# Decoder block on one core: a bias split on 16 rows, and the rounding of x1 moved from GpSimd to ScalarE

## The reference, cut to what matters

```python
def _L0_xattn_ref(q, k, v):
    ...
    scores = jnp.einsum('bkgsd,bktd->bkgst', qh, kh) / scale
    weights = jax.nn.softmax(scores, axis=-1)
    out = jnp.einsum('bkgst,bktd->bkgsd', weights, vh)
    ...
def _L0_ffn_ref(inputs, ln_w, ln_b, W1, b1, W2, b2):
    ...
    def mx_linear(x, W, b):
        y = jnp.einsum('btk,ok->bto', mx_quant(x), mx_quant(W))
        return bf16_round(y + b)
    ...
    h = mx_layernorm(x, ln_w, ln_b)
    h = mx_linear(h, W1, b1)
    h = mx_gelu(h)
    h = mx_linear(h, W2, b2)
    return bf16_round(residual + h)
x = _layernorm(x + _L0_attn_ref(x, ...), axis=-1)
x = _layernorm(x + _L0_xattn_ref(x, ctx_512, ctx_512), axis=-1)
x = _layernorm(x + _L0_ffn_ref(x, ...), axis=-1)
```

## Time and profile before

| what | value |
|---|---|
| time, median of 3 runs | 302.58 us (300.61 to 304.55) |
| the profiled execution | 303.54 us |
| its span in the trace | 301.7 us |
| busy, PE (TensorE matmuls) | 272.9 us, 90% |
| busy, DVE (VectorE) | 271.9 us, 90% |
| busy, ACT (ScalarE) | 223.0 us, 74% |
| busy, POOL (GpSimd) | 186.3 us, 62% |
| granted clock of TensorE | 1.00 of full speed |

### The profile page before, as it was taken

The page is one execution under the profiler, slowest core; times in us unless marked ns, Lnnn a source line. Parts: engine busy times, 40 slices in busy tenths (PEclk is TensorE's granted clock), DMA queues, the critical chain, the costliest instruction groups (busy, mean ns, idle before and its releaser), DMA issues.

```text
span 301.7 us, 5413 instructions
## 1 busy us (share of the span) xinstructions
PE 272.9 (90%) x1692; PEld 165.8 (55%) x1707; DVE 271.9 (90%) x665; ACT 223.0 (74%) x364; POOL 186.3 (62%) x255
## 2 busy tenths in 40 slices
PE   7898897889798999999999999999788888998887
PEld 2675556547636674667566756674346343534443
DVE  3799999999989989998999899989995999889893
ACT  4130465485898879898999899989988898875551
POOL 2829578478655768786877687767675355522321
PEclk9999999999999999999999999999999999999999
DMA  8940021102003000101210111010000000000101
GB/s 222 381 106 1 0 68 40 35 10 63 1 2 104 0 2 0 36 3 39 69 35 1 46 61 35 3 49 25 9 0 2 35 1 15 22 2 0 37 36 37
DMA packets 10067, 12.30 MB, mean 41 GB/s; under 512 B 2995, under 2 KB 7347, under 8 KB 9782
## 3 DMA queue, kind: packets, MB, share of 16 engines
q1 hardware_dynamic: 9606, 11.16, 11.9%
q10 hardware_dynamic: 432, 0.79, 0.7%
HBM read 9.85 MB, written 2.10 MB: 40 GB/s over the span
## 4 chain that ended last, share of the span: by engine, by line
PE 49%; DVE 27%; ACT 12%; issue 6%; POOL 3%; DMA 1%; DVEq 0%; POOLq 0%; ACTq 0%
PE bank L2041 9%; PE bank L2066 8%; PE bank L2079 7%; DVE am L1351 5%; DVE nm L1265 4%; PE bank L1975 3%; PE bank L2001 3%; PE bank L2145 3%; PE bank L2120 3%; ACT p_sb L848 2%; DVE wam L1351 2%; ACT xT L841 2%; ACT y_sb L862 2%; PE bank L2118 2%; ACT L848 2%
## 5 line engine op out<-in xcount | busy, mean ns | idle before, releaser
L1265 DVE TENSOR_REDUCE nm<-bank 128x4 f32<-128x512 f32 x128 | 84.1, 679 | 6.1 <-PE bank L2041 5.0
L848 ACT ACTIVATE p_sb<-bank 128x512 f32<-128x512 f32 x128 | 71.9, 599 | 13.3 <-PE bank L2066 12.5
L2041 PE MATMUL bank<-kbd,xT 96*128 96x512 f32 x128 | 57.3, 464 | 7.2 <-DVE nm L1265 4.6
L2066 PE MATMUL bank<-xT,kbd 104*128 104x512 f32 x128 | 53.7, 441 | 2.7 <-ACT p_sb L848 1.5
L543 POOL TENSOR_TENSOR kbd<-k3r,diag_sb 96x512 fp32r<-96x512 f32 x32 | 32.9, 1042 | 14.4 <-PE bank L2066 14.4
L486 POOL TENSOR_SCALAR ve<-mv 128x2 f32<-128x2 f32 (+1 forms) x36 | 12.4, 346 | 42.2 <-DVE mv L1226 37.9
L2041 PEld LDWEIGHTS bank<-kbd,xT 96*128 96x128 f32 x128 | 23.8, 188 | 23.0 <-DVE nm L1265 13.1
L2066 PEld LDWEIGHTS bank<-xT,kbd 104*128 104x128 f32 x128 | 23.5, 189 | 18.2 <-ACT p_sb L848 11.1
L2079 PE MATMUL bank<-p_sb,va_sb 128*32 128x512 f32 x256 | 32.8, 602 | 0.1
L1351 DVE TENSOR_REDUCE am<-g_sb 128x32 f32<-128x1024 bf16 x16 | 30.3, 1896 | 0.9 <-ACT g_sb L868 0.9
L841 ACT ACTIVATE xT<-bank 8x1024 fp32r<-8x1024 bf16 x16 | 16.2, 1014 | 14.9 <-PE bank L2054 14.6
(11 more groups left out here) (126 smaller groups left out, 623.4 us busy)
## 6 DMA issues: line engine op xcount, KB each, us to landing
xt_sb<-in_xt SPq DMA_DIRECT2D x8, 256.0 KB, 3.0
x_sb<-in_x SPq DMA_DIRECT2D x8, 256.0 KB, 3.1
out_dram<-o_sb SPq DMA_DIRECT2D x7, 256.0 KB, 2.2
k_sb<-in_ctx SPq DMA_DIRECT2D x8, 192.0 KB, 2.7
x_all<-in_w SPq DMA_DIRECT2D x1, 1024.0 KB, 5.7
w_raw<-in_w SPq DMA_DIRECT2D x1, 1024.0 KB, 8.0
p_sb<-in_wkv ACTq DMA_DIRECT2D x2, 256.0 KB, 4.3
cv_sb<-in_ctxv SPq DMA_DIRECT2D x8, 64.0 KB, 2.0
```

The lines of the kernel that those rows point to most:

```text
L848: sc.activation(p_sb[:, k, :], bankB[k % 2][:, :], ACT.Exp, scale=SCORE_SCALE).then_inc(s_ex, 1)
L1265: ve.tensor_reduce(nm[:, b, u, g, :], bankA[(2 + k + 11 * b) % 2][:, :].rearrange("p (k t) -> p k t", k=KU), AX.X, ALU.max, negate=True).t ...
L2041: mm(bankA[(2 + k + 11 * b) % 2][:, :], xT[0:MR, b, u, g, :], kbd[0:MR, b, u, :, :].rearrange("r k t -> r (k t)"), start=True, stop=True). ...
L2066: mm(bankB[k % 2][:, :], kbd[0:MR + 2 * KU, b, u, kk, :], xT[0:MR + 2 * KU, b, u, :, :].rearrange("r g s -> r (g s)"), start=True, stop=Tr ...
```

## The change

The bias. It is loaded as 16 rows of 80 columns in one DMA, without a wait. Four GpSimd instructions on 16 partitions by 80 columns make the three parts in `bias_parts`, early in the head. Three DMAs, issued by SP between `load_keys(2)` and `load_xt(3)`, write each part as one row of `bias_h`. The first `ffn_up` waits for these instead of for the six steps.

x1. For pairs 1 to 7 the blocks 0 and 1 of `x3` are written by two ScalarE copies, `x1_high(p, 0)` and `x1_high(p, 1)`, placed between other instructions of ScalarE. `split_x1_low` stays on GpSimd. Pair 0 is as before. A wait on `s_x2` is added to VectorE's `last_residual3`, in the last pair.

```diff
-        bias_f = sb("bias_f", [96, F + D], F32)
+        BR = 16
+        bias_f = sb("bias_f", [BR, (F + D) // BR], F32)
+        bias_rest = sb("bias_rest", [BR, (F + D) // BR], F32)
+        bias_parts = sb("bias_parts", [BR, 3, (F + D) // BR], BF16)
         bias_h = sb("bias_h", [96, F + D], BF16)
...
             def load_bias():
+                sp.dma_start(bias_f[:, :], bias.rearrange("o (r n) -> (o r) n", r=BR)).then_inc(s_w["bias"], 16)
+
+            def spread_bias():
                 sp.wait_ge(s_seta, 2)
+                sp.wait_ge(s_biasc, 4)
                 for n in range(3):
-                    sp.dma_start(bias_f[32 * n:32 * n + 1, :], bias).then_inc(s_w["bias"], 16)
+                    sp.dma_start(bias_h[32 * n:32 * n + 1, :], bias_parts[:, n, :]).then_inc(s_w["bias_rows"], 16)
...
                 load_keys(2)
+                spread_bias()
                 load_xt(3)
...
-                gp.memset(bias_f[:, :], 0.0).then_inc(s_seta, 1)
+                gp.memset(bias_h[:, :].bitcast(F32), 0.0).then_inc(s_seta, 1)
...
+            def split_bias():
+                pool.wait_ge(s_w["bias"], 16)
                 hold(pool)
+                gp.tensor_scalar(bias_parts[:, 0, :], bias_f[:, :], 1.0, 0.0, ALU.mult, ALU.add).then_inc(s_biasc, 1)
+                pool.wait_ge(s_biasc, 1)
+                gp.tensor_tensor(bias_rest[:, :], bias_f[:, :], bias_parts[:, 0, :], ALU.subtract).then_inc(s_biasc, 1)
+                pool.wait_ge(s_biasc, 2)
+                hold(pool)
+                gp.tensor_scalar(bias_parts[:, 1, :], bias_rest[:, :], 1.0, 0.0, ALU.mult, ALU.add).then_inc(s_biasc, 1)
+                pool.wait_ge(s_biasc, 3)
+                gp.tensor_tensor(bias_parts[:, 2, :], bias_rest[:, :], bias_parts[:, 1, :], ALU.subtract).then_inc(s_biasc, 1)
...
-            def split_x1_high(p, a):
-
-                if a == 0:
-                    if later(p):
-                        pool.wait_ge(s_xtp, 4 * p)
-                    pool.wait_ge(s_x1, 2 * p + 2)
-                    hold(pool)
-                gp.tensor_scalar(x3n[:, :, a, :], x1_rows(p), 1.0, 0.0, ALU.mult, ALU.add).then_inc(s_xh, 1)
...
+            def x1_high(p, a):
+                if a == 0:
+                    act.wait_ge(s_xtp, 4 * p)
+                    act.wait_ge(s_x1, 2 * p + 2)
+                sc.activation(x3n[:, :, a, :], pair_of(x_all, p).rearrange("p (n r) -> p n r", r=HR), ACT.Copy).then_inc(s_xh, 1)
...
             def last_residual3(b):
+                dve.wait_ge(s_x2, upto(LAST, b))
                 dve.wait_ge(s_s, upto(LAST, b))
...
-                        pe.wait_ge(s_biasc, 6)
+                        pe.wait_ge(s_w["bias_rows"], 48)
                         pe.wait_ge(s_seta, 5)
```

More of the change, by code:

```diff
@@ L80, in decoder_kernel @@
         w2T = sb("w2T", [P, FC, D], BF16)
-        bias_f = sb("bias_f", [96, F + D], F32)
+        BR = 16
+        bias_f = sb("bias_f", [BR, (F + D) // BR], F32)
+        bias_rest = sb("bias_rest", [BR, (F + D) // BR], F32)
+        bias_parts = sb("bias_parts", [BR, 3, (F + D) // BR], BF16)
         bias_h = sb("bias_h", [96, F + D], BF16)
-        bias_rest = sb("bias_rest", [96, F + D], F32)
-        bias_mid = sb("bias_mid", [96, F + D], BF16)
-        bias_low = sb("bias_low", [96, F + D], BF16)
         ones_b = sb("ones_b", [96, P], BF16)
@@ L199, in ffn_bank @@
             return (bankP if b == 0 else bankA)[h]
-        s_w = {k: sem(f"loaded_{k}") for k in ("wkv0", "wkv1", "wq", "wo", "tri", "ident", "diag", "ln", "w1", "w2", "bias")}
+        s_w = {k: sem(f"loaded_{k}") for k in ("wkv0", "wkv1", "wq", "wo", "tri", "ident", "diag", "ln", "w1", "w2", "bias", "bias_rows")}
         s_x = sem("x_loaded")
@@ L515, in split_xt_low @@
                 if p == 2:
-                    pool.wait_ge(s_biasc, 2)
+                    pool.wait_ge(s_rs1, PB)
                 if p == 3:
@@ L603, in head @@
                 keys_rounded(0)
-                split_bias(0)
+                split_bias()
                 split_xt_high(1)
@@ L631, in head @@
                 split_xt_low(3)
-                split_bias(3)
                 keys(1, 1, 0)
@@ L926, in head @@
                 exps(0, 0, 4)
+                x1_high(1, 0)
                 exps(0, 0, 5)
@@ L929, in head @@
                 exps(0, 0, 7)
+                x1_high(1, 1)
                 pv_copy(0, 0)
@@ L955, in head @@
                 exps(1, 0, 4)
+                x1_high(2, 0)
                 exps(1, 0, 5)
@@ L961, in head @@
                 q_copy(3)
+                x1_high(2, 1)
                 maxT(1, 1)
@@ L999, in step @@
                     v_copy(p[1], 1)
+                if on[2]:
+                    x1_high(p[2], 0)
                 if on[6]:
@@ L1004, in step @@
                     exps(p[3], 0, 4)
+                if on[2]:
+                    x1_high(p[2], 1)
                 if on[5]:
@@ L1072, in tail @@
                 exps(6, 0, 3)
+                x1_high(7, 0)
                 gT_copy(4, 0)
@@ L1075, in tail @@
                 exps(6, 0, 5)
+                x1_high(7, 1)
                 exps(6, 0, 6)
```

36 lines of the change are left out of this document (removed).

## The result

The changed kernel takes 308.22 us, the median of 4 runs (306.44 to 311.34), against 302.67 us for the kernel before in the same measurement. The ratio is 1.0195 with a 95% interval of 1.0136 to 1.0254. The forecast was 303.8 us, with a range up to 306.3: the change is slower than forecast, by more than the range allowed. By the measure of 2% it stays undecided whether it counts as slower, for the interval lies on both sides of 1.02; that it is slower than before is clear. A second measurement of the same code gave 307.99 us and a ratio of 1.0183 (1.0129 to 1.0238).

What follows compares the result with a forecast made beforehand. In a step TensorE, VectorE and ScalarE were taken to run nearly in lockstep; in the head VectorE was full. -1.5 us (head) + 2.7 us (steps) = +1.2 us gave 303.8 us, range 299.4 to 306.3 us.

Steps and rivals of the forecast that it cites:

- the race: In three steps GpSimd's subtraction starts just before VectorE's `gz` and holds it: `gz` 1.4 us instead of 0.42.
- The `wz` pair: In the head near 49 us, two VectorE instructions freed of `bias_low` take 1.3 us instead of 3.71.
- Pair 7: In the tail, `gz` starts before GpSimd's subtraction is released, and GpSimd's `kbd` waits for TensorE anyway: no cost.
- The second copy's 0.5 us: In a step, ScalarE's second copy of x1, behind `exps` 4, lies in ScalarE's waits for TensorE: no cost.
- Pairs 1 and 2 fall in ScalarE's slack in the head.: In the head, moving x1 of these pairs to ScalarE costs nothing.
- The third pair's input comes earlier, not later: In the head, SP's three new DMAs cost at most 1.3 of 3 us gained before `load_xt(3)`: no cost.
- rival 4: Another GpSimd instruction falls on the head's two `wz`, the head gains nothing: +2.7 us, 305.3 us; chance 0.10.
- the head's 1.5 us: In the head, without `bias_low` TensorE goes on at 52.45 us instead of 53.94; 1.5 us gained, carried through unchanged.
- the 0.09 us: In a step, the margin by which GpSimd's subtraction (131.87 us) starts ahead of `gz` (131.96 us); called the weakest term.
- 0.8 us a step: TensorE's lateness in each of three steps from held `gz`, late `exps` included; 2.4 us in all.
- The part of the late `exps`: In a step, ScalarE's first copy delays `exps` 3, making TensorE 0.23 us late, in three steps.
- the third, ScalarE as the bound: Each of four steps takes both copies in full, the head gains nothing: +6.3 us, 308.9 us; chance 0.06.

Runs made afterwards that it cites:

- the bias part alone: The changed kernel with both copies of x1 back on GpSimd at their old places: 301.4 us, ratio 0.9955; on repeat 300.59 us, 0.9969.
- x1 alone: The kernel before with its old bias split kept and the two ScalarE copies of x1 added: 311.74 us, ratio 1.0314.
- the two versions that turn the race round: The changed kernel with ScalarE's first copy moved behind `norm4`, 306.48 us; or with GpSimd's subtraction moved behind the third norm's `rs`, 305.89 us.

## Why the prediction was wrong

**Right.** The reading of the race was. GpSimd's subtraction was to start at 131.87 us; it started at 132.04, which is 131.84 with the 0.20 us by which that step began late. That it came so close is in part luck: the copy took 0.65 us instead of 0.61 and the release 0.08 instead of 0.14, and the two misses cancel. `gz` was to take 1.4 us and took 1.44, in all three steps, and the first step's subtraction was put at 101.35 us and came at 101.04, which is 101.30 without that step's 0.26 us of lead. The `wz` pair was to take 1.3 us and took 1.29. Pair 7 was to cost nothing, and its `gz` took 0.42. The second copy's 0.5 us were to lie in a wait, and do. The four small bias steps, bounded by 1.2 us, took 1.15 us. The three issues on SP, however, took 1.83 us against a bound of 1.3.

**Wrong: "Pairs 1 and 2 fall in ScalarE's slack in the head."** This step failed most. I looked at the engine that receives the work, and not at what moves up on the engine that loses it. Two copies fewer let GpSimd's keys and its subtraction for `xt` start at 45.34 and 46.52 us, over the two `win` ahead of `m_all`; before it was 46.57 and 47.75, over `m_all` and the last `win`, and with the bias part alone 49.22 and 50.39, behind `wz`. And its `k3r` comes over `xb_all`. Against the bias part alone it costs 1.8 us (95.67 against 93.87 us). With the old bias split, x1 alone makes the head 3.7 us slower than the kernel before. "The third pair's input comes earlier, not later" was right and was taken for harmless. For the head I had named rival 4, another GpSimd instruction on the two `wz`; the holds are on their neighbours, where they had been before, and later on `xb_all` and `wqb`.

**Mis-sized: the head's 1.5 us.** The bias part alone gives 1.97 us at the first table load, 2.18 counted from the first `maxima`. The missing part is on the way to TensorE ahead of `wz`: `m_all`, 0.92 us in the kernel before and 0.19 now, and a `win` ahead of it, 0.61 and 0.15, of which I hadn't asked whether they were held. With x1 moved too, 1.09 us reach TensorE (1.35 counted so), and 0.26 us (0.52) are left: the carried gain was the term that I had called weak next to the 0.09 us.

**Mis-sized: 0.8 us a step.** It is 1.0. The part of the late `exps`, 0.23 in the forecast, is 0.35 without any hold and 0.6 with that of `m_all`, and `gz` adds the rest. So the two effects don't add up as I added them.

**Missing: `hq` in the second step, 1.0 us.** I knew that `s_sb` and `hq` start close, but only in the tail; in the steps they start 0.23 us apart. Why GpSimd's second `h_sb` came 0.3 us late in this step alone was not tried, and stays open. The held `hq` shows in both profiles of the changed kernel, and in no experiment with half of the change. The late `h_sb` shows in one place more: in the same step of the two versions that turn the race round (0.43 and 0.44 us behind the first), which have almost the same list of GpSimd instructions. In the steps of all the other profiles it is 0.13 to 0.15 us. So it doesn't come from the held `gz`, and it costs the 1.0 us only together with that hold. The bias part alone has a delay of the same size at another place, its copy of x1 in the second step (0.29 us).

**Missing: the clock, 1.4 us in this execution.** It was seen only behind a held `hq`, and not behind each.

Of the rivals, the third, ScalarE as the bound, gave 308.9 us and comes nearest to the time. That is luck. Its mechanism, ScalarE as the bound, is refuted: ScalarE's waits before `pv_sb` and `exps` are 2.2 and 2.0 us where they were 2.2 and 1.6, and moving one GpSimd instruction, with ScalarE's work unchanged, took 0.4 to 0.65 us off each of the last three steps. A number that fits is no proof of the reason that produced it.

## What to carry to other kernels

When work leaves an engine, list what moves up behind it, and hold the new start times against those of the engine that it can hold (here GpSimd and VectorE hold each other); the receiving engine's slack is the smaller question. An instruction whose own time is 0.2 us can stand for 2.6 us if a long one starts 0.01 us ahead of it, so the short instructions that lie beside long ones, and starts within 0.3 us of each other, are the terms to look for, and every shift, also an earlier load, can turn them. Look too at which are held already: here `m_all` and two `win` were, in the kernel before. And change one thing at a time: here the bias part was a gain of some 0.3 to 0.45% in two measurements, neither of which has an interval wholly below 1, and the x1 part hid it under 2%.
